# Column attention on one Trainium2 core: the row sums of a group's two halves in one run over four column tiles

## The reference, cut to what matters

```
Q, K, V = X@Wq+bq, X@Wk+bk, X@Wv+bv        # each reshaped to (N, 16 heads, 256, 8), Q scaled
scores  = einsum('neax,nebx->neab', Q, K)
A       = softmax(scores, axis=2)          # over a, for each b
Out     = einsum('neab,neax->neax', A, V)  # only the sum over b of A is needed
return Out.reshape(N, 256, 128) @ Wo + bo
```

## Time and profile before

| What | Value |
|---|---|
| median of 3 runs | 1831.04 us (1827.69 to 1834.07) |
| profiled execution | 1828.47 us, its span 1826.7 us |
| PE busy | 1696.1 us, 93% |
| DVE busy | 1373.4 us, 75% |
| ACT busy | 1313.0 us, 72% |
| POOL busy | 1125.1 us, 62% |
| first and last exp of column attention (line 1875) | 878.5 and 1131.2 us from the span's start |

### The profile page before, as it was taken

How to read it: one execution, slowest core, us unless ns; L and a number is a source line. 1 busy time by engine, 2 the same in 40 slices (tenths; PEclk the granted TensorE clock), 3 DMA queues, 4 the chain that set the end, 5 groups by cost and what they waited for, 6 DMA issues and landing times. The chain is left out here.

```text
span 1826.7 us, 43522 instructions
## 1 busy us (share of the span) xinstructions
PE 1696.1 (93%) x15560; PEld 1104.3 (60%) x15560; DVE 1373.4 (75%) x2360; ACT 1313.0 (72%) x4482; POOL 1125.1 (62%) x1011
## 2 busy tenths in 40 slices
PE   7998899999889999999799999799999899999999
PEld 4664577775557777655344444467776556777655
DVE  4553899994679999546788886699995588999645
ACT  4444688887348888745799998688888437888853
POOL 3553899994379999602322121799996278999730
PEclk8998999999999999999899999999999999999999
DMA  2002111102011110201756651211102102110201
GB/s 64 2 2 56 24 28 32 26 19 71 26 25 35 31 25 19 53 15 26 125 91 102 98 93 30 69 28 30 25 19 54 49 1 54 25 31 19 46 22 44
DMA packets 71453, 74.80 MB, mean 41 GB/s; under 512 B 17652, under 2 KB 55240, under 8 KB 69192
## 3 DMA queue, kind: packets, MB, share of 16 engines
q1 hardware_dynamic: 71240, 72.03, 19.1%
HBM read 27.99 MB, written 10.49 MB: 21 GB/s over the span
## 5 line engine op out<-in xcount | busy, mean ns | idle before, releaser
L428 POOL TENSOR_TENSOR rsum<-pa,pb 128x512 f32<-128x512 f32 x256 | 324.7, 1288 | 55.6 <-DVE pa L346 37.2
L807 ACT ACTIVATE ffn_prob<-sc,ffn_nmax 128x128 f32<-128x128 f32 x928 | 327.6, 387 | 5.7 <-DVE ffn_nmax L728 5.7
L894 POOL TENSOR_TENSOR ffn_prob<-ffn_prob,ffn_rden 128x512 f32<-128x512 f32 x256 | 265.3, 1057 | 70.5 <-DVE ffn_rden L738 70.3
L437 POOL TENSOR_TENSOR rsum<-rsum,ffn_rnt 128x512 f32<-128x512 f32 x256 | 261.5, 1042 | 10.9 <-ACT ffn_rnt L829 8.6
L807 ACT ACTIVATION_READ_ACCUMULATOR ffn_prob<-sc,ffn_nmax 128x1 f32 x928 | 210.3, 227 | 0.0
L356 DVE TENSOR_TENSOR pb<-proj,ffn_tab 128x512 f32<-128x512 f32 x236 | 161.6, 685 | 59.4 <-ACT rn L398 58.8
L336 PE MATMUL pt<-ident,rsum 128*128 128x128 f32 x960 | 154.7, 285 | 14.8 <-POOL rsum L437 12.0
L336 PEld LDWEIGHTS pt<-ident,rsum 128*128 128x128 f32 x960 | 101.3, 141 | 96.0 <-ACT ffn_ptb L815 70.4
L728 DVE TENSOR_REDUCE ffn_nmax<-sc 128x4 f32<-128x512 f32 x232 | 148.5, 681 | 14.4 <-PE sc L622 11.6
L365 DVE TENSOR_REDUCE ffn_ss<-rn 128x16 f32<-128x1024 f32 x128 | 154.7, 1209 | 0.0
L632 PE MATMUL pt<-ident,ffn_prob 128*128 128x128 f32 x1024 | 143.2, 278 | 11.3 <-POOL ffn_prob L894 10.9
(11 more groups left out here) (275 smaller groups left out, 4380.7 us busy)
## 6 DMA issues: line engine op xcount, KB each, us to landing
ffn_v<-ffn_v SPq DMA_DIRECT2D x128, 128.0 KB, 2.3
column_ks<-qk_parts SPq DMA_DIRECT2D x64, 128.0 KB
rn<-Y SPq DMA_DIRECT2D x32, 128.0 KB, 2.3
qk_parts<-column_hi SPq DMA_DIRECT2D x64, 64.0 KB, 1.7
qk_parts<-column_lo SPq DMA_DIRECT2D x64, 64.0 KB, 1.7
column_qs<-qk_parts SPq DMA_DIRECT2D x32, 128.0 KB
column_qs<-qk_parts SPq DMA_DIRECT2D x64, 64.0 KB
rn<-Y SPq DMA_DIRECT2D x32, 127.5 KB, 2.4
```

The source lines that it names most:

```text
L428: pool.tensor_tensor(K.sm[:, r, w], K.m1[:, r, w], K.m2[:, r, w], ALU.add).then_inc(S.f_sum, 1)
L437: pool.tensor_tensor(heads(K.sm[:, r, w]), heads(K.sm[:, r, w]), K.rnt[:, r, w * HEADS:(w + 1) * HEADS].unsqueeze(2).broadcast_to([P, HEAD ...
L807: ins = act.activation(K.prob[:, r, e, k], score_banks(i)[e][:, tokens(k)], ACT.Exp, bias=K.nmax[:, r, e, k:k + 1], accum_out=K.den[:, r, ...
L894: pool.tensor_tensor(K.prob[:, r, e], K.prob[:, r, e], K.rden[:, r, e].unsqueeze(2).broadcast_to([P, 4, P]), ALU.mult).then_inc(S.f_pn, 1)
```

## The change: what it does

`row_sums` loses its half. It now runs once for a group: eight matmuls, bt outside and c = 0 to 3 inside, over all four column tiles, with one wait for the inverses of both halves and one semaphore step. In PE's order it stands behind `scores` of both halves and ahead of the product and the piece of the sequence before. The waits of `inverses`, `take` and of the exp count groups instead of halves.

More of the change, by code:

```diff
@@ L1686, in scores, with row_sums @@
                     mm.then_inc(S.b_sc, 1)
-            def row_sums(q, G, h):
-                if q == 0 and G == 0 and h == 0:
+            def row_sums(q, G):
+                if q == 0 and G == 0:
                     pe.wait_ge(S.b_zero, 2)
-                pe.wait_ge(S.b_rd, 8 * q + 2 * G + h + 1)
-                if G == 0 and h == 0 and q >= 2:
+                pe.wait_ge(S.b_rd, 8 * q + 2 * G + 2)
+                if G == 0 and q >= 2:
                     pe.wait_ge(S.b_rc, q - 1)
                 for bt in range(2):
-                    for c in B_HALVES[h]:
+                    for c in range(4):
                         mm = pe.matmul(row_banks[q % 2][32 * c:32 * c + 4, 0:SEQ], B.rd[:, G, c, bt], B.E[:, 4 * (G % 2) + c, bt],
@@ L1741, in _ @@
                     scores(q, G, 0)
+                    scores(q, G, 1)
                     if before[0] >= 0:
-                        row_sums(*before, 0)
-                    scores(q, G, 1)
+                        row_sums(*before)
                     g = (q + 3) // 2
@@ L1752, in _ @@
                         (turn, spread, project)[G - 1](q - 1)
[L1753 to L1756, removed]
+            row_sums(SEQS - 1, 3)
             turn(SEQS - 1)
@@ L1780, in inverses @@
                 if q >= 1:
-                    dve.wait_ge(S.b_rs, 8 * (q - 1) + 2 * G + h + 1)
+                    dve.wait_ge(S.b_rs, 4 * (q - 1) + G + 1)
                 k = 4 * (G % 2) + h
@@ L1785, in take @@
             def take(q):
-                dve.wait_ge(S.b_rs, 8 * q + 8)
+                dve.wait_ge(S.b_rs, 4 * q + 4)
                 if q >= 1:
@@ L1872, in _ @@
                             if n == 0 and (q or G >= 2):
-                                act.wait_ge(S.b_rs, 8 * q + 2 * G + h - 3)
+                                act.wait_ge(S.b_rs, 4 * q + G - 1)
                             for bt in range(2):
```

## The result

The changed kernel takes 1877.53 us (median of 4 runs, 1868.19 to 1883.61) against 1830.74 before: ratio 1.0259, 95% interval 1.0225 to 1.0293. It is slower by 2.6%, far outside the range of 1824 to 1842. The profiled execution is the longest of the four, 1883.61 us with a span of 1881.7.

A forecast was written before the change was run, and what follows sets the result against it. The prediction took ACT to set column attention's pace, with PE paying only through ACT's waits; its terms summed to +0.6 us on the 1831.04 median, giving 1831.6 us, range 1824 to 1842.

The forecast's parts named there:

- the one on the clock: Column attention: PE busy share falls to 69%, clock stays unchanged; a fall to 1.2 GHz was a slower rival, chance 0.04.
- Its price: Cost if the stage's clock falls to 1.2 GHz: 43 us, so 1875; some 1842 if a quarter does; chance 0.04.
- What bounds the stage: Column attention: ACT sets the pace, a freely running group takes 3.61 us; only 15.2 us of ACT's waits lie within.
- The run: Row sums over four column tiles: 16 records in 1.07 us, holding PE for 1.00 instead of 1.94.
- The rival of a longer hold: Every group: row sums hold PE longer than 1.00, 5.1 us for each 0.1; 1837 to 1879; chance 0.10.
- G 0 to G 1: Distance between the groups' first exps: 4.17 us against 4.40, DVE's keep now late; 12 times, -2.8 us.
- G 1 to G 2 of odd sequences: Distance between first exps: 5.11 us against 4.26, as DVE now waits for the turn; 6 times, +5.1 us.
- G 2 to G 3: Distance between first exps: 4.00 us against 4.15, through spread and weigh; 12 times, -1.8 us.
- Free groups: Groups that ran freely: 3.64 us against 3.60, 18 times 0.04, +0.8 us; rival of slipping more, chance 0.04.
- The order's sum: All terms of the new order: -2.8 + 5.1 - 1.8 - 0.3 + 0.8 - 0.4 = +0.6 us.
- the 20.2 us of slips: Column attention before the change: group distances beyond 3.60 us, summed over 12 sequences that have products.
- the first rival: Faster: PE handed on sooner, hold 0.89, about 1826.5 us; ceiling with every slip gone -20.2 us or 1811; chance 0.16.

The follow-up runs named there:

- the second half held back: Changed kernel, but the second half's four row-sum matmuls wait on a semaphore for the first half's end; 1926.1 us, ratio 1.0524.
- the full-clock run above: Changed kernel plus two float32 matmuls whose result nobody reads in every group; 1836.1 us, ratio 1.0030, clock 1.00.

## Why the prediction was wrong

- **The failed step is the one on the clock:** "So the nearest row speaks for an unchanged clock". I set the busy share of a stretch (7.23 of 10 us at 1.00) against the share that I expected, 69%. The clock in the stage came to 0.67, which the prediction had named as a sign of being wrong. The busy share is the wrong quantity. Kernels of this case had 167.65 us of 183 busy at 0.79, 145.83 at 0.67 and, with the second half held back, only 136.53 at 0.89. A PE record is longer than the time until the next one on the same tile starts: in the full-clock run above each lasts 0.38 us, and the next on its tile starts 0.22 after it started; so the union of records says little of how much work stands in it. The change halves the row sums' hold, from 1.94 to 0.97 us in each group. The Trainium skill ("TensorE: Matmul & The Clock Gate", the part on the clock gate), weighed there and set aside, says that activity releases the throttled clock. The trace agrees so far that the clock fell to 0.67 when PE's work went down. I gave it 0.04.
- **Its price came out near by luck.** "0.85 x 51 = 43 if all of the stage goes so, 1875"; measured 1877.53. Two errors cancel. The clock was at the lower level only part of the time, and the slow groups lost more than the run's 0.85, since spread lost 0.95 (2.08 against 1.13; 6.08 against 4.0 us of distance) and the product some 0.7 as well (1.65 us at 1085.61, against the 0.98 of the earlier trace rows).
- **What bounds the stage: right at full clock only.** With the clock held at 1.00, groups without a wait still take ACT's 3.6 us. In the changed kernel ACT waits 73.4 us for maxima, and DVE 39.6 us for spread alone.
- **The run: right.** 1.05 us and a hold of 0.97, forecast 1.07 and 1.00. The rival of a longer hold falls.
- **G 0 to G 1: right,** 4.13 for 4.17. **G 1 to G 2 of odd sequences: right,** 5.02 for 5.11, with the new wait for the turn. **G 2 to G 3: right in even sequences,** 4.01 for 4.00, **wrong in odd ones,** 4.17, no less than before.
- **Free groups: right.** 3.62 for 3.64 in the changed kernel. With the added work the distance into G 2 of even sequences is 3.77, so the rest is that work's.
- **The order's sum: +0.6 put down, measured +3.3 us in the stage** (256.0 against 252.7, profiled) or 1.0030 of the whole, in the kernel with the clock held up by added work. By term, forecast and then measured: into G 1 -2.8 and -1.8 (4.27, where it is 4.13 without added work in the group), into G 2 of odd sequences +5.1 and +4.5, into G 3 -1.8 and -0.6, sequences 13 to 15 -0.3 and 0, free groups +0.8 and +0.9, start -0.4 and +0.2.
- **A reading of the trace before:** the 20.2 us of slips left out those into G 3 of sequences 13 to 15, where the distance is 4.05 (1.35 us in all). The ceiling of the first rival would have been lower by that; the sum of +0.6 doesn't use it.

That the clock is the cause of the slowdown, and PE's lighter work a cause of the clock's fall, is shown from both sides: putting work back takes 41 of 47 us away, and taking work out of the kernel before, with nothing moved, lowers its clock and makes it slower. That the order costs only a few microseconds at full clock is shown as well, though with the added work in it. It costs more through the clock: with the run last in G 1 to G 3 the same work on PE keeps 0.81 instead of 0.67. How the clock's fall divides between less work, its order and the waits within a group is open.

## What to carry to other kernels

When a change makes PE's work shorter in a stage that another engine paces, little is won on PE and, as here, the clock can be lost; price that case with the cold durations of the same instructions and give it weight, and don't read it off the busy share. Test it by doing the removal alone, without the reordering, and by adding back matmuls whose result nobody reads. If the added work helps, look for an order in which less waits behind it, and don't add it to a kernel whose PE is already late: here 92 matmuls of 0.43 us, some 40 us, cost 43.

## What the runs showed of the hardware that was not expected

- Taking two of four matmuls from each half of the row sums, with order and waits unchanged, lowered the granted clock from 1.00 to 0.79 and made the kernel 0.5% slower, while PE's busy time (167.65 against 170.18 us of 183) and its longest idle gap (0.83 us in both) hardly changed.
- The same PE work in another order got another clock: 0.67 with the run ahead of the product and turn, spread or project, 0.81 with it behind them in G 1 to G 3.
- Matmuls in four column tiles overlap in both orders that were tried: 16 records in 1.05 us as c = 0, 1, 2, 3 and in 1.06 as 0, 2, 0, 2, 1, 3, 1, 3; held apart by a semaphore they take 2.13.
